# Windowed attention and a LoRA-style feed-forward layer on one core: mask rows inside 128-row score stacks, and the softmax shared by three engines

## What is computed

```
q, k, v = (x @ W + b) split into 16 heads of 8 channels
scores  = q @ k.T / sqrt(8)                       # per head
allowed = (j <= i) & (i - j < 32)                 # causal, window of 32
attn    = softmax(where(allowed, scores, -1e30))
out     = (attn @ v) @ Wo + bo
h       = gelu(x @ W1.T + scale * (x @ m1.T) + b1)
y       = h @ W2.T + scale * (h @ m2.T) + b2
```

## Time and profile before

| | us |
|---|---|
| median of 3 runs | 146.55 |
| the profiled execution | 145.36 |
| its span | 143.6 |
| TensorE busy (matmul) | 110.2 (77%) |
| VectorE busy | 96.1 (67%) |
| ScalarE busy | 68.9 (48%) |
| GpSimd busy | 46.2 (32%) |
| mean share of the 16 DMA engines on the main queue | 49.4% |
| mean granted TensorE clock | 0.952 of full |

### The profile page before, as it was taken

The page is one execution under the profiler, slowest core; times in us unless marked ns, Lnnn a source line. Parts: engine busy times, 40 slices in busy tenths (PEclk is TensorE's granted clock), DMA queues, the critical chain, the costliest instruction groups (busy, mean ns, idle before and its releaser), DMA issues.

```text
span 143.6 us, 6819 instructions
## 1 busy us (share of the span) xinstructions
PE 110.2 (77%) x2888; PEld 78.5 (55%) x2888; DVE 96.1 (67%) x254; ACT 68.9 (48%) x157; POOL 46.2 (32%) x67
## 2 busy tenths in 40 slices
PE   0368619579846959966868768587699999999992
PEld 0235505357634746844646546475455649595891
DVE  1571508998697979967969979999999551111031
ACT  3125604556466357445738639438724772433300
POOL 3473360739424006006005103602900299200000
PEclk9999986857999996899999999999999999999999
DMA  1699693946697866596655595491000000202022
GB/s 40 172 324 275 183 333 110 302 120 184 158 262 199 242 183 181 142 286 195 202 175 155 167 293 141 109 258 36 0 5 0 5 2 0 79 1 69 4 73 73
DMA packets 39734, 20.60 MB, mean 143 GB/s; under 512 B 1431, under 2 KB 39582, under 8 KB 39710
## 3 DMA queue, kind: packets, MB, share of 16 engines
q1 hardware_dynamic: 39710, 20.26, 49.4%
HBM read 10.82 MB, written 9.44 MB: 141 GB/s over the span
## 4 chain that ended last, share of the span: by engine, by line
PE 37%; DMA 21%; DVE 18%; issue 10%; SPq 5%; ACT 4%; DVEq 1%; POOL 1%; ACTq 0%
DMA KS<-k_scr 14%; PE bank_o L466 6%; DVE probsT L774 5%; PE bank_qk L584 5%; PE bank_s L489 5%; PE bank_v L584 4%; PE bank_o L489 4%; DMA k_scr<-k_parts 3%; SPq L227 3%; DVE negmax L759 3%; DVE centred L766 2%; DMA q_scr<-q_parts 2%; PE bank_s L443 2%; PE bank_w L512 2%; SPq L210 2%
## 5 line engine op out<-in xcount | busy, mean ns | idle before, releaser
L466 PE MATMUL bank_o<-V,probsT 128*32 128x36 f32 x1024 | 24.9, 206 | 13.1 <-DVE probsT L774 12.4
L654 ACT ACTIVATE probs<-centred 128x512 f32<-128x512 f32 x32 | 20.2, 631 | 26.2 <-DVE probsT L774 17.3
L466 PEld LDWEIGHTS bank_o<-V,probsT 128*32 128x32 f32 x1024 | 21.3, 118 | 18.3 <-issue 13.7
L759 DVE TENSOR_REDUCE negmax<-bank_s 128x8 f32<-128x512 f32 x32 | 21.6, 676 | 8.2 <-PE bank_s L443 8.2
L774 DVE STREAM_TRANSPOSE probsT<-probs 128x512 f32<-128x512 f32 x32 | 22.4, 699 | 0.0
L766 DVE TENSOR_TENSOR centred<-bank_s,negmax 128x512 f32<-128x512 f32 x32 | 21.2, 663 | 0.2
L269 POOL TENSOR_TENSOR q_parts<-rest,q_parts 128x256 bf16<-128x256 f32 x8 | 5.4, 672 | 43.2 <-ACT q_parts L601 43.2
L443 PEld LDWEIGHTS bank_s<-KS,QS 64*32 64x32 bf16 x1024 | 10.3, 98 | 13.2 <-issue 13.2
L436 PE MATMUL bank_s<-masks,ident_bf 128*128 128x512 bf16 x31 | 13.1, 423 | 3.9 <-DMA KS<-k_scr 2.4
L443 PE MATMUL bank_s<-KS,QS 64*32 64x64 bf16 x1024 | 14.6, 199 | 1.6 <-issue 1.6
L601 ACT ACTIVATE V<-bank_v 32x256 f32<-32x256 f32 x32 | 11.9, 371 | 0.4
(11 more groups left out here) (98 smaller groups left out, 200.3 us busy)
## 6 DMA issues: line engine op xcount, KB each, us to landing
QS<-q_scr SPq DMA_DIRECT2D x8, 512.0 KB, 4.2
KS<-k_scr SPq DMA_DIRECT2D x7, 576.0 KB, 5.9
q_scr<-q_parts SPq DMA_DIRECT2D x16, 192.0 KB, 3.0
k_scr<-k_parts SPq DMA_DIRECT2D x16, 192.0 KB, 3.1
q_scr<-q_parts SPq DMA_DIRECT2D x8, 128.0 KB, 3.0
k_scr<-k_parts SPq DMA_DIRECT2D x8, 128.0 KB, 2.2
x_sb<-in_L_attn_x_dram SPq DMA_DIRECT2D x1, 768.0 KB, 5.6
out_dram<-y SPq DMA_DIRECT2D x3, 256.0 KB, 2.3
```

The costliest lines, as they stand in the source:

```text
L466: mm = nc.tensor.matmul(o[q * WIN:(q + 1) * WIN, g * VC:(g + 1) * VC], probsT[s % 2][:, i, g, w, :], V[b][:, j + w, g, :], start=(w == 0), ...
L654: nc.scalar.activation(probs[s % 2][:], centred[s % 2][:].rearrange("p a k -> p (a k)"), ACT.Exp, scale=float(HD) ** -0.5).then_inc(probs_ ...
L759: nc.vector.tensor_reduce(negmax[s % 2][:], bank_s[s % 2][:].rearrange("p (a k) -> p a k", k=2 * WIN), AX.X, ALU.max, negate=True).then_in ...
```

## The change

- **Mask rows in the stacks.** The parts now use 6 slots (high x high, middle x high, low x high, high x middle, middle x middle, high x low), so a head needs 48 rows. Each head has a stack of 128 rows of its own: QS and KS get a dimension `odd`, with the head's 48 rows in one half of the partitions, and in the other half the rows of the mask: a 64x64 identity in QS and a band of 0 and -1e30 in KS. VectorE writes them once for each buffer (`fill_q`, `fill_k`, `fill_pad`). The scores are then 32 matmuls of 128 rows with nothing laid below them: L436 and L432 are gone. QS and KS are read by two DMAs each a chunk.
- **The softmax shared.** ScalarE copies the bank into `logits` in SBUF, VectorE takes the maximum from there, GpSimd adds the negated maximum, ScalarE takes the exponential as before. The bank is free once it is copied.
- **The order.** TensorE's step starts with scores(s+1), ahead of values(s-3). turn_x and xT move from u = 1 to u = 0, project and high from u = 2 to u = 1, middle from u = 3 to u = 2. VectorE's step starts with turn_probs(s-2) and split_rest, then row_max(s). GpSimd's step starts with subtract_max(s); at u = 3 follow the normalisation of chunk c+3 and the low parts of chunk c+2. GpSimd's loop over turns is written out.
- **The start.** tri is made otherwise and the band matmuls come first on TensorE; the memsets of V stand after the low parts of chunks 0 and 1.

More of the change, by code:

```diff
@@ L96, in block_kernel @@
         half = sb("half", [P, NT])
[L98 to L100 removed]
+        tri = sb("tri", [WIN, 2, 6, WIN])
+        bands = sb("bands", [P, 2, 2 * WIN], BF16)
         in_quad = sb("in_quad", [P, GH])
@@ L299, in _ @@
-            for first in range(2):
-                nc.gpsimd.affine_select(out=tri[:, first], in_=tri[:, first], compare_op=ALU.is_ge, fill=NEG, base=WIN,
-                                        pattern=[[-1, 2 * WIN]], channel_multiplier=1).then_inc(consts, 1)
+            for row in range(2):
+                for own in range(2):
+                    at = tri[:, row, (1 - own) ^ row:6:4]
+                    nc.gpsimd.affine_select(out=at, in_=at, compare_op=ALU.is_ge if own else ALU.is_gt, fill=NEG, base=0,
+                                            pattern=[[0, 2], [-1 if own else 1, WIN]],
+                                            channel_multiplier=1 if own else -1).then_inc(consts, 1)
@@ L302, in _ @@
+            ln1_rstd(1, 0, TILES)
             ln1_rstd(2, TILES, 2 * TILES)
-            for b in range(2):
-                nc.gpsimd.memset(V[b][:, :, :, 0:GH * HD], 0.0).then_inc(v_set, 1)
             low_parts(0, 0)
+            nc.gpsimd.memset(V[0][:, :, :, 0:GH * HD], 0.0).then_inc(v_set, 1)
             ln1_rstd(3, 2 * TILES, 4 * TILES)
             low_parts(0, 1)
+            nc.gpsimd.memset(V[1][:, :, :, 0:GH * HD], 0.0).then_inc(v_set, 1)
             nc.gpsimd.affine_select(out=shift[:], in_=ones[:], compare_op=ALU.is_equal, fill=0.0, base=1,
@@ L372, in body @@
                     step(turn, s, is_last(turn))
-            turns(pool, body)
+            pool.wait_ge(rstd1_done, 3)
+            ln1_norm(2, 0)
+            for turn in range(SUPER):
+                body(turn)
             for f in range(2, NF):
@@ L413, in project_v, with spread_bands @@
                 mm.then_inc(v_ps, 1)
-            def spread_masks():
+            def spread_bands():
                 pe.wait_ge(consts, 6)
-                for hh in range(GH):
-                    mm = nc.tensor.matmul(bank_w[hh * WIN:(hh + 1) * WIN, 0:4 * WIN], ident[0:WIN, 0:WIN],
-                                          tri[:].rearrange("p n k -> p (n k)"), start=True, stop=True)
+                for quad in range(GH):
+                    e = quad % 2
+                    row, first = (0 if e else 1), (2 if quad < 2 else 0)
+                    mm = nc.tensor.matmul(bank_w[quad * WIN:(quad + 1) * WIN, 0:4 * WIN], ident[0:WIN, 0:WIN],
+                                          tri[:, row, first:first + 4].rearrange("p n k -> p (n k)"), start=True, stop=True)
                 mm.then_inc(masks_ps, 1)
@@ L519, in step @@
                 tiles = SU // 2
+                if s + 1 < SU:
+                    scores(turn, s + 1)
+                elif s + 1 == SU and not last:
+                    scores(turn + 1, 0)
                 if not (first and s < 3) and s < SU + 3:
@@ L527, in step @@
                     c = 2 * turn + b
+                    if p1 and u == 0:
+                        turn_x(c + 2, b)
                     if p1 and u == 1:
-                        turn_x(c + 2, b)
-                    if p1 and u == 2:
                         project(c + 2, b)
-                if s + 1 < SU:
-                    scores(turn, s + 1)
-                elif s + 1 == SU and not last:
-                    scores(turn + 1, 0)
-                if s < SU:
                     if not (last and b == 1) and u == 2:
@@ L696, in step @@
                 if s < SU:
-                    if p1 and u == 3:
+                    if p1 and u == 2:
                         middle(c + 2, b)
@@ L859, in step @@
                 outs = s % 2 == 1 and not (first and s < 5) and s < SU + 4
+                if not (first and s < 2) and s < SU + 2:
+                    turn_probs(turn if s >= 2 else turn - 1, (s - 2) % SU)
+                if s < SU and p1 and u == 2:
+                    split_rest(2 * turn + b + 2, b)
                 if rows:
@@ L868, in step @@
                     denominators(out_tile, (s - 5) // 2 % 2)
-                if s < SU:
-                    subtract_max(turn, s)
-                if s < SU and p1 and u == 2:
-                    split_rest(2 * turn + b + 2, b)
                 if first and s == 0:
                     ln1_var(4 * TILES, NT)
-                if not (first and s < 2) and s < SU + 2:
-                    turn_probs(turn if s >= 2 else turn - 1, (s - 2) % SU)
+                if first and s == 2:
+                    fill_pad(0).then_inc(filled, 1)
                 if s % 2 == 1 and not (first and s < 7):
```

95 lines of the change are left out of this document (46 added, 49 removed).

## The result

The changed kernel takes 152.81 us, the median of 4 runs (152.04 to 153.62), where the kernel before, run beside it, takes 146.75 (146.3 to 147.8). The ratio is 1.040, with a 95% interval of 1.032 to 1.049. The forecast was 141.2 with a range to 149: wrong in sign and outside the range. The profiled execution took 153.3, its span is 151.5. Medians here are of all executions of a kernel, ratios only of those near its fastest, and the profiled executions of e1, e7, e8, e12 and e16 are slower ones that the ratios leave out.

A forecast was written before the change was run, and what follows sets the result against it. The prediction took the restack loop through DRAM to bind at 20.7 us per two chunks. Start 20.5, chunks 20.7 + 1.1, 20.7, 20.7, 10.35 and tail 44.2 gave 138.2 of span, 141.2 us as measured; range 133 to 149.

The forecast's parts named there:

- The doubt of the Trainium skill: TensorE scores: weight loads would not overlap with same rows, so a unit costs 0.7, total some 2 us more.
- the first part of the loop: From scores of chunk c to low parts of c+2: 13.2 us taken, ends 12.5 and 14.0, against 11.8 before.
- long end: First part of the loop at 14.0 us: the stack stall also holds values, and ScalarE's high parts wait 1.5.
- The second part: From low parts to landed stacks: 7.5 us taken, ends 6.5 and 8.8, against 10.5 before.
- The clock: Sign against the forecast: a granted clock under 0.78 over two chunks.
- Nobody's busy time holds the old pace; what remains is the loop: Chunks 4 and 5: engines at 12.6 to 17.3 busy out of 21.6 us, so the loop binds.
- Rival B: Loop hides; ScalarE's 17.3 us of work with gaps binds at 18.4 for two chunks: 133.2 us, chance 0.22.
- The start: Before the first scores: fills cost time, fewer bytes save some; scores start at 20.5 instead of 21.0.
- D: VectorE's fills at the dear end (5.0 and 6.3 us) delay the start: 146 to 149 us, chance 0.10.
- The end: After chunk 7's first scores: 44.2 us for 45.2, ends 43 and 46.
- C: GpSimd's in-order queue: low parts wait behind subtraction and normalisation, later than 14.8 us; total 152.1, chance 0.18.
- E: Loop stays at 22.3, low parts losing what transfers gain; only chunk 6 gains: 145.5 to 147 us, chance 0.08.

The follow-up runs named there:

- e1: Changed kernel with the next unit's scores again behind values, output projection, turn_x and projection on TensorE: 151.31 us, 1.027 of the kernel before.
- e7: Changed kernel with softmax unshared, second buffer's fills behind the split of chunk 1, low parts first on GpSimd, scores ahead of values: 147.22 us, 1.004.
- e8: Changed kernel with softmax unshared, second buffer's fills late, low parts first on GpSimd, scores behind values and projections: 144.04 us, 0.985 of the kernel before.
- e12: Kernel before the change with only the next unit's scores moved ahead of the values on TensorE: 152.39 us, 1.021 of the kernel before.
- e16: Changed kernel with two of GpSimd's first-turn additions of bo to x moved behind the low parts: 150.1 us, 1.016 of the kernel before.
- e6: Kernel before the change with only the softmax shared (ScalarE copies, GpSimd subtracts), 64-row scores and old order kept: 153.11 us, 1.046.
- e11: Changed kernel with 12 throwaway matmuls on TensorE ahead of each stack wait but the first: 150.16 us, 1.016 of the kernel before.
- e5: Changed kernel with softmax unshared: VectorE does maximum and subtraction from the bank, no ScalarE copy: 149.97 us, 1.029 of the kernel before.
- e3: Changed kernel with the second buffer's fills moved behind the split of chunk 1 on VectorE: 151.11 us, 1.034 of the kernel before.
- e4: Changed kernel with 1.06 us of memsets added on GpSimd right ahead of the low parts: 155.49 us, 1.068 of the kernel before.
- e2: Changed kernel with GpSimd's low parts at unit 3 ahead of the subtraction, normalisation last: 152.34 us, 1.043 of the kernel before.
- e17: Changed kernel with two bo additions behind the low parts and, at unit 3, the normalisation behind them too: 151.3 us, 1.026.
- e18: Changed kernel with two bo additions behind the low parts and the second buffer's fills behind the split of chunk 1: 149.94 us, 1.021.
- e14: Unshared kernel with late fills, low parts first and scores behind values, plus 12 throwaway matmuls ahead of each stack wait but the first: 150.42 us, 1.028.

## Why the forecast was wrong

**What held.** The prices did: copies 0.600 (0.591 forecast), subtractions 1.04, maxima 0.67, a unit of 128-row scores 0.42 at full clock (0.4 taken). The doubt of the Trainium skill (TensorE: Matmul & The Clock Gate, Part 3: Packing small matmuls), by which it would have been 0.7, is not borne out: 0.42 at 128 rows stands against 0.40 at 64 rows, and the mean of a score matmul is 218 ns at 128 rows and 205 at 64 (e6), both over mixed clocks. VectorE's load per two chunks is 13.6 to 14.3 (13.1 forecast), ScalarE's 15.3 to 16.5 (17.3), GpSimd's after the first turn 12.4 to 13.2 (12.6). Chunks do wait for a stack each time, though for 1.2 to 4.4 us and not 0.5 to 1.5.

**The step that failed first: the first part of the loop, 13.2 us, long end 14.0.** From a chunk's scores to the end of the low parts of the chunk after next it was 13.5, 16.2, 15.2, 15.1, 13.5 and 13.2. (Its short end was mis-added too: 8.4 and 4.3 are 12.7, not 12.5.) The sum put 4.3 us behind ScalarE's copy: maximum, subtraction, normalisation, low parts. It had the additions to x_bo only as load of the first two chunks, 1.1 us together with two weight copies, and not as a wait in front of the low parts. The two that count are 1.28 and 2.35 us in GpSimd's queue, ahead of two subtractions and two pairs of low parts; a third, 1.27 at 41.21, fits in ahead of its next maximum. From chunk 0 to 2 the loop took 21.4 (21.8 forecast), from chunk 1 to 3 it took 26.2. In the old kernel the additions cost nothing, since GpSimd waited 4.72 us for its input behind them:

```profile
33.93 3.60 POOL L276 TENSOR_TENSOR x_bo<-x_sb,bo_row 128x512 f32<-128x512 f32 x2
42.24 0.67 POOL L269 TENSOR_TENSOR q_parts<-rest,q_parts 128x256 bf16<-128x256 f32 x1 [4.72 <-ACT q_parts L601]
```

Once it carries the subtraction, they are on the path. e16 prices this place at 2.4%. And the long end gave the wait with the scores ahead 1.5 us, for ScalarE's high parts alone. It stops VectorE too (19.1 us of waits), by the output projection, which costs about 1.3% here (e1) and 2.1% in the old kernel (e12). The stretches behind the waits of 3.2 to 4.4 us are mostly the long ones, 16.2, 15.2 and 15.1; behind chunk 5's wait of 4.23 came only 13.2, where no normalisation stood ahead of the low parts.

**The second part, 7.5, ends 6.5 and 8.8**, was 7.9, 10.1, 9.8, 8.0, 8.1 and 8.7. The chain of waits gives its pieces, for chunks 3 and 5 (start, length, what):

```profile
48.94 3.02 DMA q_scr<-q_parts
...
53.41 6.07 DMA KS<-k_scr
```

```profile
74.06 1.54 DMA q_scr<-q_parts
...
77.07 5.47 DMA KS<-k_scr
```

The last stack took 4.8 to 6.3 us over chunks 2 to 7, on both sides of the 5.4 of the sum. The writes of the low parts, 1.9 in the sum, took 1.5 to 1.6 us in chunks 2, 5, 6 and 7 and 2.6 to 3.2 in chunks 3 and 4, the two that have the stretches of 10.1 and 9.8. With 128 KB they had taken 2.1 to 3.5 in the same chunks of the old kernel. So half the bytes did make most of these writes faster; why two of the six took twice as long as the others stays open. This part was mis-sized by 0.4 to 2.6 us a loop, about as much in all as the first part.

**The clock was in no term.** I wrote only that under 0.78 would be a sign against the forecast. Chunks 2 and 3 stood at 0.74. A wait of TensorE costs its own length and, in the stretch behind, the difference between 0.62 and 0.42 a unit; e11 pays 12 matmuls a chunk and still gains 2.4%. It fits, too, that taking off what I had put at 7 us of masks brought only 3.3 of busy time.

**"Nobody's busy time holds the old pace; what remains is the loop"** was a false choice. Something else can bound, with no engine full and hardly a stack late (e6, 12.0 us a chunk), and by exclusion it is the chain of hand-overs. Rival B's text had the gaps in it, as an argument against B, but gave them 1 us. Sharing alone makes the old kernel 4.6% slower. In the changed kernel it costs about 1.1% (e5), perhaps because the loop is slow beside it.

**The start, -0.5, was +3.6.** The fills were cheaper than forecast and D is out. What cost is the exclusion that the forecast had cited for two other places. The low part of q beside the fills took 2.80, and 0.67 without them (e3); here the trace agrees with the Trainium skill (SBUF — State Buffer, SBUF: two separate sides). I looked for neighbours of the memsets and of the added subtractions, and not for who else runs beside the fills. It was also the cheapest error: undone, it brings 0.6 to 0.9%, and nothing that shows after e16.

**The end, -1.0, was +1.7.** By e11, whose end takes 45.3 at a granted clock of 1.00 where the changed kernel has 46.9 at 0.94, the 1.7 are clock. The forecast 1.0 of gain does not come at full clock either.

**The rivals.** C had the sign, and its price of 152.1 is the nearest to 152.8. That nearness is luck in part: C has the scores of chunk 7 at 104.9 and they started at 104.58, but from a start 4.1 us later than C's and with loops 4.4 us shorter in all, and the end was 2.7 longer. Its mechanism is shown for GpSimd's queue: the low parts passed its deciding point of 14.8 us in chunks 1 to 3, and e4 and e16 move the time at that place in both directions. But it blamed subtraction and normalisation, where moving them gained nothing, since TensorE then waited for the normalised chunks (e2, e17), and not the bias additions, where moving two does gain. And it is a part: the order of the scores (e12), the clock (e11) and the sharing (e6) each have an experiment of their own that is clear of noise. The singles (e1 1.3%, e3 0.7%, e5 1.1%) sum to 3%, while with e2's edit all together bring 5.3% (e8): that fits a stretch with several bounds close together, which gives little to who relieves one, though three of these singles are near or within noise. E's idea was nearest for chunks 4 and 5, at 21.6 in both kernels.

**What stays open**: which hand-over of the shared softmax is the slow one (e6), why the start's 2.9 us die in the first turn even with GpSimd's queue cleared (e18), and what TensorE's gaps are in which it waits for nothing that the profile shows. Between 20 and 110 us of the profiled executions such gaps of over 0.7 us come to 1.3 us in the kernel before and 3.0 in the changed one, but to 8.5 in e5 and 11.0 in e8; so what an edit frees can be lost in them, and the singles may understate their causes.

## What to carry to other kernels

Before an engine is given work because it is idle, list all that already stands in its in-order queue: what cost nothing while the engine waited is on the path from then on. An instruction that may wait belongs behind work that is ready, and a wait of TensorE is to be priced with the clock of what follows. Busy times that all fall below the span prove no gain; count the hand-overs per unit of work and try them by themselves first. When an instruction is moved back in a queue, look for who waits for it now.

## What the runs showed of the hardware

- A GpSimd operation on two tensors took 2.80 instead of 0.67 us beside consecutive bfloat16 copies of VectorE, while the copies kept their 0.65 and 0.42. GpSimd bore the whole cost, and ended about 0.7 us after the last of the 1024-element copies.
- Bfloat16 copies with a repeated source ran at 0.32 ns an element (0.65 for 2048) and 0.41 (0.42 for 1024), a quarter to a third of the 1.22 that I had drawn from the earlier trace rows.
- Twelve matmuls whose results are thrown away ahead of each wait held the granted clock at 1.00 in the profiled run (e11). With many such waits the kernel was 2.4% faster for it, with few 4% slower (e14).
- The write of a low part, 64 KB, took 1.5 to 1.6 us in four chunks of the loop and 2.6 to 3.2 in two, where 128 KB had taken 2.1 to 3.5.
